# Chunk 2's head products after the last h-gate quarter, and its row scaling around the last root

## The reference, cut to what matters

```python
for _ in range(5):
    a_in  = A @ (state @ in_W.T + in_b)
    a_out = A.T @ (state @ out_W.T + out_b)
    a = concatenate([a_in, a_out, state], -1)
    r = sigmoid(a @ r_W.T + r_b)
    z = sigmoid(a @ z_W.T + z_b)
    h = tanh(concatenate([a_in, a_out, r * state], -1) @ h_W.T + h_b)
    state = (1 - z) * state + z * h
out = tanh(state @ o1_W.T + o1_b) @ o2_W.T + o2_b
y = x + out
return (y - mean(y)) / sqrt(var(y) + 1e-5)      # over the 256 features of a row
```

## Time and profile before

| | us |
|---|---|
| median of 3 runs | 982.41 (980.74 to 984.47) |
| the profiled execution's own time | 983.18 |
| its span in the trace | 981.4 |
| TensorE busy | 961.5 (98%) |
| VectorE busy | 765.5 (78%) |
| ScalarE busy | 469.7 (48%) |
| GpSimd busy | 41.8 (4%) |
| mean granted TensorE clock | 0.997 of full speed |

### The profile page before, as it was taken

The page is one execution under the profiler, slowest core; times in us unless marked ns, Lnnn a source line. Parts: engine busy times, 40 slices in busy tenths (PEclk is TensorE's granted clock), DMA queues, the critical chain, the costliest instruction groups (busy, mean ns, idle before and its releaser), DMA issues.

```text
span 981.4 us, 12040 instructions
## 1 busy us (share of the span) xinstructions
PE 961.5 (98%) x4507; PEld 443.3 (45%) x4507; DVE 765.5 (78%) x1202; ACT 469.7 (48%) x663; POOL 41.8 (4%) x57
## 2 busy tenths in 40 slices
PE   7999999999999999999999999999999999999996
PEld 3444444444444444444444444444444444455445
DVE  4989989888888688867867876787677787745756
ACT  4657566554345346433634553364335435422444
POOL 0310100000000000000000000000000000031101
PEclk9999999999999999999999999999999999999998
DMA  9999995234730455194025607701571482042101
GB/s 335 364 410 362 378 347 150 59 81 103 209 85 1 120 156 101 38 208 131 0 77 153 146 1 166 189 22 33 155 167 22 102 215 65 16 135 86 44 1 44
DMA packets 199787, 134.36 MB, mean 137 GB/s; under 512 B 62257, under 2 KB 191921, under 8 KB 195761
## 3 DMA queue, kind: packets, MB, share of 16 engines
q1 hardware_dynamic: 197424, 125.20, 44.8%
q0 software_dynamic: 2304, 8.39, 2.2%
HBM read 102.11 MB, written 16.78 MB: 121 GB/s over the span
## 4 chain that ended last, share of the span: by engine, by line
PE 79%; DMA 9%; ACT 5%; DVE 4%; issue 2%; SPq 1%; ACTq 0%; DVEq 0%
PE bank L1960 36%; PE bank L2101 19%; PE bank L2079 11%; PE bank L2093 6%; DMA tmp<-in_adj_t 5%; DMA tmp<-in_adj 4%; PE bank L2109 3%; ACT areg L616 3%; PE bank L2174 1%; PE bank L2196 1%; PE bank L2158 1%; PE bank L1885 1%; SPq L413 0%; ACT pq_words L631 0%; ACT areg L811 0%
## 5 line engine op out<-in xcount | busy, mean ns | idle before, releaser
L1960 PE MATMUL bank<-areg,xop_words 128*128 128x512 fp8e4 x1792 | 389.5, 379 | 0.8 <-DVE pq_words L1496 0.8
L1960 PEld LDWEIGHTS bank<-areg,xop_words 128*128 128x128 f16 x1792 | 174.9, 98 | 213.0 <-DVE pq_words L1496 2.7
L811 ACT ACTIVATE areg<-pq_words 128x512 f16<-128x512 f32 x90 | 56.3, 629 | 163.5 <-DVE pq_words L1496 62.5
L2101 PE MATMUL bank<-areg,pq_words 128*128 128x512 f16 x504 | 122.7, 379 | 0.3 <-DVE pq_words L1607 0.3
L1885 PE MATMUL bank<-areg,xop_words 128*128 128x512 fp8e4 x512 | 112.1, 379 | 4.1 <-ACT areg L616 2.1
L2101 PE MATMUL bank<-areg,w 128*128 128x512 f16 x378 | 90.7, 379 | 0.0
L1532 DVE SCALAR_TENSOR_TENSOR areg<-pq_words,areg 128x512 f16<-128x512 f32 x90 | 62.2, 691 | 32.4 <-ACT areg L811 30.6
L1885 PEld LDWEIGHTS bank<-areg,xop_words 128*128 128x128 f16 x512 | 49.7, 98 | 65.5 <-issue 4.2
L616 ACT ACTIVATE areg<-tmp 128x2048 fp8e4<-128x2048 int32 x31 | 59.2, 1915 | 38.2 <-DMA tmp<-in_adj_t 21.4
L2101 PEld LDWEIGHTS bank<-areg,pq_words 128*128 128x128 f16 x504 | 49.2, 98 | 60.1 <-issue 0.8
L2079 PE MATMUL bank<-pq_words,w 128*128 128x512 f16 x288 | 65.4, 379 | 0.0
(11 more groups left out here) (247 smaller groups left out, 1260.1 us busy)
## 6 DMA issues: line engine op xcount, KB each, us to landing
areg<-kept_operands SPq DMA_DIRECT2D x112, 512.0 KB, 4.3
tmp<-in_adj_t SPq DMA_DIRECT2D x16, 1024.0 KB, 8.2
tmp<-in_adj SPq DMA_DIRECT2D x15, 1024.0 KB, 7.7
kept_operands<-xop_words POOLq DMA_DIRECT2D x11, 512.0 KB, 8.1
kept_operands<-areg SPq DMA_DIRECT2D x4, 1024.0 KB, 10.2
areg<-in_x SPq DMA_DIRECT2D x7, 512.0 KB, 4.8
kept_operands<-tmp POOLq DMA_DIRECT2D x5, 512.0 KB, 3.2
pq_words<-in_gate_w SPq DMA_DIRECT2D x6, 384.0 KB, 5.7
```

What stands on the lines that cost most here:

```text
L811: nc.scalar.activation(y_dst(t, g, name)[:, 0, :], src, ACT.Copy, scale=PSC).then_inc(s_yh, 1)
L1960: last = nc.tensor.matmul(dst[:, :], xop[:, m // 2, operand_block(xo, part, m % 2), :], place8[:, mo, m, :], start=first and m == pairs[0] ...
L2101: last = nc.tensor.matmul(dst[:, :], weights(d, wp), yop[:, d, Y_PLACE[name], xp, :], start=False, stop=final and gate < 2 and d == 1 and ...
```

## The change

The output products of chunk 2 (`head_out(2)`) move from behind tile 3 to behind the four quarters of gate h. Two PSUM place functions change with it (`last_hidden(1)` writes the banks 0 and 1, chunk 3's head rows lie in the banks 4 to 7), and the wait for `s_qact` 4 moves from `last_out(1)` to `last_out(0)`. On VectorE the work on chunk 2's rows moves behind the quarters' updates: two row blocks before and two after the last state split, its statistics, aggregate and first root between the hidden quarters' low parts. On ScalarE a square root of one element of a constant is added behind the last hidden quarter; two of chunk 2's row blocks are scaled before the square root of chunk 3's variances and two after it.

```diff
         def last_hidden_bank(h, m):
-            return bank[((4, 7), (2, 3))[h][m]]
+            return bank[((4, 7), (0, 1))[h][m]]

         def head_rows(c, j):
             if c == CH - 1:
-                return bank[(0, 1, 5, 6)[j]][:, 0:D]
+                return bank[4 + j][:, 0:D]
@@ ScalarE
             last_hidden(3)
+
+            nc.scalar.activation(ln_t[:, 5, 0:1], SIG, ACT.Sqrt)
+
+
             act.wait_ge(s_rstd, 1)
-            for j in range(JC):
-                normalize_act(CH - 2, j)
-
-
+            normalize_act(CH - 2, 0)
+            normalize_act(CH - 2, 1)
             act.wait_ge(s_var, 2)
             nc.scalar.activation(ln_t[:, 5, JC:], ln_t[:, 0, JC:], ACT.Sqrt).then_inc(s_root, 1)
+            normalize_act(CH - 2, 2)
+            normalize_act(CH - 2, 3)
             act.wait_ge(s_rstd, 2)
@@ VectorE
             def last_updates():
+                for i in range(3):
+                    last_update(i)
+                    last_split_lo(i)
+                last_update(3)
                 add_rows(2, range(JC // 2))
+                last_split_lo(3)
+                add_rows(2, range(JC // 2, JC))
                 statistics(2, 0)
                 statistics(2, 1)
-                add_rows(2, range(JC // 2, JC))
+                last_hidden_lo(0)
                 statistics(2, 2)
                 stats = statistics(2, 3)
-                last_update(0)
+                last_hidden_lo(1)
                 ln_link(stats)
                 aggregate(range(JC))
-                last_split_lo(0)
+                last_hidden_lo(2)
                 first_root()
-                last_update(1)
-                last_split_lo(1)
-                last_update(2)
-                last_split_lo(2)
-                last_update(3)
-                last_hidden_lo(0)
-                last_split_lo(3)
-                for i in range(1, 4):
-                    last_hidden_lo(i)
+                last_hidden_lo(3)
@@ TensorE
             def last_out(h):
-                if h == 1:
+                if h == 0:
                     pe.wait_ge(s_qact, len(QUARTERS))
...
                     if t == LAST and c == CH - 1 and gi == 2:
                         head_hidden(2)
-                    if t == LAST and c == CH - 1 and gi == 3:
-                        head_out(2)
...
             for i in range(len(QUARTERS)):
                 last_gate(i)
+            head_out(2)
             for h in range(2):
                 last_hidden(h)
```

## The result

| | before | changed |
|---|---|---|
| median, us (22 runs each, side by side) | 981.15 | 984.16 |
| lowest to highest | 979.85 to 986.11 | 982.86 to 987.23 |
| ratio, 95% interval | | 1.0028 (1.0018 to 1.0038) |
| span of the profiled execution | 981.4 | 981.4 |

The kernel became 0.28% slower, 2.75 us at this median (the two medians lie 3.01 us apart). The forecast was +2.95 us, 985.4 against a median of 982.41 from three runs.

A forecast was written before the change was run, and what follows sets the result against it. TensorE bounds the kernel up to chunk 3's head, then hand-overs between engines; late GpSimd and scalings +2.90 us plus stores 0.05 make +2.95 on 982.41, forecast 985.4 us, range 983.2 to 988.0.

The forecast's parts named there:

- TensorE: nothing gained: TensorE around tile 3's end: quarters come 2.62 us earlier, but chunk 3's hidden products still start at 966.6 us.
- The last split, and the hold: Last state split stays at 969.1 us behind ScalarE's `last_hidden(0)`; VectorE's queue waits 2.7 us idle for it.
- the prediction's own rival without the hold: VectorE's queue not held at the split, its high part being early: +1.3 us, 983.7 us; chance 0.04.
- VectorE's queue: VectorE's work behind the split: last hidden low part at 973.76 instead of 972.12, chunk 3's variance 1.65 us late.
- GpSimd: GpSimd's Newton chain for chunk 2 starts at 973.93, ten us later, runs without slowing, ends last at 977.94.
- the 722 ns row: Earlier GpSimd addition beside a PSUM-and-SBUF VectorE addition, taken as the sign that Newton operations would not be slowed.
- The rival with GpSimd slowed as before: Row blocks and statistics slow GpSimd's chain to its earlier 5.27 us: 1.26 us more, 986.6 us; chance 0.2.
- ScalarE: ScalarE's end: table load covered, 4.4 us wait for GpSimd, last two scalings 2.34 us after it, +2.90 us.
- second load: Rival on ScalarE: scalings need another table, two more loads after GpSimd's end, +5.5 us, 987.9 us; chance 0.03.
- Stores: Closing stores on SyncE: chunk 2's now run just ahead of chunk 3's, adding 0.05 us (0 to 0.3).
- No longer than before: Rival: adjacency loads of the first 230 us come 3 us or more earlier, median at or under 982.4; chance 0.06.
- The clock rival: TensorE's clock halves for the last six products, at most 0.65 us, covered by 1.3 us slack; no chance given.

The follow-up runs named there:

- experiment 1: Changed kernel with chunk 2's 24 head products back behind tile 3, all other orders as changed; tail 13.52 us (13.54 changed, 10.92 before), ratio 1.0023.
- experiment 2: Changed kernel with VectorE's list alone altered: chunk 2's rows and statistics ahead of the last split, aggregate and first root one low part earlier; tail 11.31 us, ratio 1.0000.
- experiment 3: Changed kernel with the last split's high part ahead of the first hidden quarter's tanh in ScalarE's list; tail 11.45 us, ratio 1.0011.
- experiment 4: Changed kernel with one of GpSimd's three Newton steps for chunk 2's root; tail 13.39 us in the first profile, 12.28 in the second, ratio 1.0018.
- experiment 5: Changed kernel without the added one-element root on ScalarE; tail 14.94 us, ratio 1.0034.
- experiment 6: Changed kernel with ScalarE's end as before: no added root, all four scalings of chunk 2 ahead of the root; tail 15.92 us, ratio 1.0056.

## Why the prediction was right, step by step

- **TensorE: nothing gained.** Right; experiment 1 puts the move at 0.02 us.
- **The last split, and the hold.** The high part kept its place 2.10 us after the first hidden product, and VectorE idled 2.78 us for the 2.7 forecast. Experiments 2 and 3 show that the loss comes from VectorE's order together with the late high part: undoing either gives back 2.1 to 2.2 of the 2.62 us. How much of it is the hold itself isn't isolated, since each edit frees something more. The estimate in experiment 2 has 1.2 us for it, which would leave +1.4 us; the prediction's own rival without the hold was +1.3.
- **VectorE's queue.** The last hidden low part was put at 973.76, 7.30 us after the first hidden product; it came at 7.02. The mis-sized term is the hidden low part's hold of VectorE: I took 0.41 us to the next start, the distance from L1353 to L1346 in the earlier trace rows; ahead of a statistics instruction it was 0.33 (968.25 to 968.58). Three of them make 0.24 of the 0.28 us by which the forecast's +2.90 exceeded the tail's +2.62.
- **GpSimd.** The chain was put at 4.01 us and took 4.03. The choice of the 722 ns row as the nearest was right (the 16 additions of that line have a median of 724 ns): the twelve operations beside row blocks, statistics and aggregate took 0.19 to 0.20 us, and the one beside a low part, with two inputs in SBUF, 0.30. With that the Trainium skill's rule ("SBUF — State Buffer", "Who interferes with whom") holds for the statistics too, for which no row of before spoke. The rival with GpSimd slowed as before, +1.26 us, is out.
- **ScalarE.** It waited 4.12 us where 4.4 were forecast, the table load was covered, and from the end of GpSimd's chain (975.00) to the last scalings went 2.32 us for the 2.34. No second load appeared. That GpSimd hides VectorE's lateness is shown by experiment 4: 1.36 us without it. The prediction had this as 1.65, too much by nearly the same 0.28.
- **Stores.** From the start of the last scalings to the end of the span it is 4.02 us before and 4.08 after: 0.06 us for the forecast's 0.05. In the stretches of after (columns as in the earlier trace rows) the last three stores run into each other, at a DMA share near 1 from 978.2 to 980.2 us:

```profile
977.80:978.20 0.40, 0.00 (x0) 0.00 (x0) 0.13 (x1) 0.40 (x2) 0.00 (x0) 0.50 0.21 69
978.20:978.60 0.40, 0.00 (x0) 0.00 (x0) 0.00 (x0) 0.20 (x1) 0.00 (x0) 0.50 1.07 358
...
979.80:980.20 0.40, 0.00 (x0) 0.00 (x0) 0.00 (x0) 0.00 (x0) 0.00 (x0) 0.50 0.96 335
```

- **The sum.** +2.95 forecast, +2.68 by the profile (2.62 and 0.06), +2.75 by the ratio, with 0.98 us to either side. The forecast lay 1.2 us above the measured 984.16, all of it from the median before: 982.41 in the three runs that I went by, 981.15 in 22. "A measurement of this kernel can tell about 0.5%" was too cautious: 22 runs of each kernel told 0.28% from nothing, with 0.10% to either side.
- **The other rivals.** "No longer than before" didn't come: the adjacency loads moved the rest by 2.72 us in the profiled execution, enough to make the spans equal, but not in the median of 22. The clock rival I had called free of cost. In the changed kernel's profile it didn't occur (TensorE's pause was 1.03 us for the 1.3 forecast). It did in one experiment, and for all 24 last products, not the six I had reckoned with. There, without GpSimd's cover, it cost 13.39 - 12.28 = 1.11 us, more than the 0.65 I had as the most. By that number the 1.3 us of cover in the changed kernel would still have held it; "no case of its own" leaned on that.

## What to carry to other kernels

An engine's list holds whatever stands behind a wait, so before work is put around a wait, ask when that wait is really met: here the new state of the last quarter was ready some 3 us earlier against the first hidden product (the instruction that writes it starts 1.37 us ahead of it, before the change 1.59 us behind it), and its split was still released at the old time, by another engine's list. A chain on a slow side engine is free only as long as its start isn't moved; GpSimd had 2.8 us to spare, and its start moved by 9.7 (from 2.5 us ahead of chunk 3's first hidden product to 7.2 behind it). And when two executions are compared, measure from an event that both share just ahead of the change: the equal spans hid the whole effect.

## What the runs showed of the hardware

In one of the eleven profiles (the first of experiment 4) TensorE's clock fell to 1.2 GHz at about 971.1 us, just as the last 24 products began (971.05), and rose again at about 974.5. TensorE had been busy up to 968.2, then it had one pause of 1.04 us, six products, and another pause of 1.03 us. The same kernel in its other profile, the changed kernel, and experiments 1, 5 and 6 had the same two pauses and kept 2.4 GHz through the 24 products, which took 3.29 us in each. I can't say from these runs what decides it; it cost the last 24 products 1.15 us.
